# Mamba block on one core: a convolution tap and the carried columns on VectorE, x copied by ScalarE, two of sixteen products on GpSimd, jobs placed anew

## The chip, the cores and the metric

One core of a Trainium2 chip. The metric is the device time of one execution in microseconds (us), from the core's first to its last instruction and what lies around it. Names: TensorE (PE, its weight loads PEld), VectorE (DVE), ScalarE (ACT), GpSimd (POOL), SyncE (SP, which issues all DMAs of the part discussed here).

## What is computed

The program runs layer norms, a two-layer Mamba block, a slot-routing feed-forward, windowed attention and the feed-forward again, on two sequences of 2048 tokens with 256 features. Only the Mamba block is touched. Cut to what matters:

```
xc, z = split(x @ in_w.T)                                    # 512 + 512 features
xc = silu(sum(xp[:, k:k+L] * cw[:, k] for k in range(4)) + cb)   # causal convolution, 4 taps
dt, B, C = split(xc @ xp_w.T)                                # 16, 16, 16
dt = softplus(dt @ dtp_w.T + dtp_b);  A = -exp(A_log)
h[t] = exp(dt[t] * A) * h[t-1] + (dt[t] * xc[t]) * B[t]      # 512 features x 16 states
y[t] = sum_n h[t] * C[t] + xc[t] * D;  out = (y * silu(z)) @ out_w.T
```

## The kernel before

The Mamba part (function `mamba`) works in 16 steps: 2 layers x 2 sequences x 4 chunks of 512 tokens. The 512 x 16 states of a chunk are cut into 64 **units** of 128 partitions (32 features x 4 states) x 512 tokens. For each unit `u`, in this order on each engine:

- ScalarE makes `decay` = exp(A dt) (`decay`, L522; four slots, so it may lead the scans by four units).
- TensorE transposes four 128x128 blocks of `u_B` = (dt x) B into one of two PSUM banks (`inject`, L755).
- VectorE scans over the 512 tokens (`scan`, L406), from `decay` in SBUF and the bank in PSUM, into one of 12 slots of `h`. The scan of unit k of a later chunk begins with column k of `h_carry`.
- GpSimd multiplies the slot by the C rows (`output`, L624).
- TensorE sums the states of four units, a **quad**, into a PSUM bank (`states`, L764), 11 units behind.

`u_B` itself comes from 16 products per 16 units (`product`): 13 on ScalarE (L545) and 3 on GpSimd (L613).

All other work of a step is hung between the units. Each engine's program is one loop `for k in range(UNITS)`, and tuples at the head of the file say behind which unit a job stands: `D_...` for VectorE, `A_...` ScalarE, `G_...` GpSimd, `P_...` TensorE. In step s (p = s + 1) these jobs finish step s-1 (gate, out projection, residual) and prepare the inputs of step s+1 in one chain: norm, transposed features, `project_x`, copy of x out of PSUM (L482), convolution (three taps as products with diagonal weights on TensorE, L678; the newest tap and the sum on VectorE, L350), SiLU (L493), x_proj (L708), `dt_B_C` copy (L507), dt products (L726), softplus (L511, L514), then for four token blocks the transposes of x (L735) and dt (L744), the copy of x to `u_tok` (`tok_x`, L372) and its product with dt (`tok_u`, L377). ScalarE needs a table load (ACT_TABLE_LOAD) when it turns between exp, SiLU and softplus.

After each quad ScalarE copies the four last columns of the scans' slots to `h_carry` (`keep`, L530); GpSimd waits for this copy before it overwrites the quad. All order between engines is by semaphores; each engine takes its instructions strictly in the written order.

Of the kernel before, what the change touches and what calls it, by code (L numbers as in the profile page):

```python
# [63 lines left out]
D_GATE = (62, 63, 4, 7)  # L64
D_RES = (13, 16)
D_STATS = (6, 6, 6, 10)
D_MEAN = 11
# [8 lines left out]
A_NORM = 15
A_FEAT = 20
A_X = (25, 28, 34, 39)
A_PROJ = 43
# [1 line left out]
D_RAW = (11, 12, 13, 14, 28, 38, 39)
G_PROD = (0, 4, 7)
G_RSTD = 5
P_Z = (0, 1, 2, 4, 5, 6, 6, 7)
P_SKIP = (0, 11, 12, 17)
P_OUT = (9, 9, 10, 11, 13, 14, 15, 16)
P_FEAT = 18
P_X = (20, 21, 22, 23, 29, 31, 32, 33)
# [43 lines left out]
def mamba(nc, x, r, weights, consts):  # L132
# [7 lines left out]
    with ExitStack() as ctx:  # L140
# [65 lines left out]
        with nc.Block() as block:  # L206
# [101 lines left out]
            def _(dve):  # L308
# [37 lines left out]
                def conv(p, ct):  # L346
                    at(dve, "conv_mm", CT * p + ct + 1)
                    if ct == 0:
                        at(dve, "skip_mm", CT * p)
                    dve.scalar_tensor_tensor(xc[:, ct], xs[:, ct, DC - 1:], kc(p, K_CW, ct * DC + DC - 1),  # L350
                                             PS[:, conv_bank(p, ct)], ALU.mult, ALU.add).then_inc(S["conv"], 1)
# [1483 lines left out]
```

## Time and profile before

| | |
|---|---|
| median of 3 runs | 2516.12 us (2514.9 to 2517.61) |
| profiled execution, its own time | 2518.79 us |
| its span, first to last instruction | 2517.0 us |
| busy in the span | TensorE 87%, VectorE 75%, ScalarE 72%, GpSimd 64% |
| mean granted TensorE clock | 0.956 of full speed |

In the profile a line names engine, source line, operation, the tile written and the tiles read. Records of TensorE's 512-column fp32 products come in pairs, two to a product. The number at a row's start in a timeline is its start in us from the span's start, the next its length; "x4" means four instructions merged, the length is then that of all four together. "[0.29 <-PE psum L755]" is idle time ahead of it and what ended it.

### The profile page before, as it was taken

How to read it: one execution, taken by the hardware profiler on the slowest of the kernel's cores; microseconds unless marked ns; L12 is line 12 of the kernel's file. 1: busy time of each engine (PE TensorE's matmuls, PEld its weight loads, DVE VectorE, ACT ScalarE, POOL GpSimd, SP SyncE). 2: the span in 40 equal slices, each digit the busy share in tenths (PEclk: the TensorE clock that was granted, in tenths of full speed). 3: DMA queues.
4: the chain of work that ended last, by engine and by line, in shares of the span. 5: the costliest groups of instructions: out<-in, count | busy, mean ns of one | idle time of the engine just before them, and what ended most of it. 6: DMA issues, size and time to landing. Idle time of an engine off the chain costs nothing. (4 is left out here: it accounts for less than half of the span.)

```text
span 2517.0 us, 40372 instructions
## 1 busy us (share of the span) xinstructions
PE 2185.7 (87%) x14544; PEld 1308.8 (52%) x14544; DVE 1895.6 (75%) x2590; ACT 1819.2 (72%) x3103; POOL 1619.7 (64%) x1410
## 2 busy tenths in 40 slices
PE   5789899898998989889898898986368699999967
PEld 2445455454554545545455454553134477787844
DVE  5688889888898888988889898898374455555553
ACT  2888998889989889888888989887252244444452
POOL 1689889898898988989889898899210411231010
PEclk9899999999999999999999999999578799999988
DMA  5540414314143240432404224040501211110031
GB/s 169 123 106 22 118 43 93 96 32 118 42 94 87 78 118 30 114 77 51 118 16 119 66 61 111 17 118 9 190 1 62 65 33 33 29 33 25 21 116 67
DMA packets 129787, 183.73 MB, mean 73 GB/s; under 512 B 14002, under 2 KB 75954, under 8 KB 129204
## 3 DMA queue, kind: packets, MB, share of 16 engines
q1 hardware_dynamic: 129588, 181.16, 26.8%
q8 instruction: 115, 1.88, 0.3%
q14 instruction: 84, 0.69, 0.1%
HBM read 134.45 MB, written 42.47 MB: 70 GB/s over the span
## 5 line engine op out<-in xcount | busy, mean ns | idle before, releaser
L624 POOL TENSOR_TENSOR h<-h,C_rep 128x512 f32<-128x512 f32 x1024 | 1275.9, 1283 | 202.4 <-ACT h_carry L530 202.4
L406 DVE TENSOR_TENSOR_SCAN h<-decay,h_carry,psum 128x512 f32<-128x512 f32 x768 | 955.8, 1270 | 126.4 <-PE psum L755 93.6
L522 ACT ACTIVATE decay<-dt_rep,A 128x512 f32<-128x512 f32 x1024 | 729.3, 713 | 103.6 <-DVE h L406 93.0
L755 PEld LDWEIGHTS psum<-ident,u_B 128*128 128x128 f32 x4096 | 479.1, 142 | 562.5 <-DVE h L406 310.3
L755 PE MATMUL psum<-ident,u_B 128*128 128x128 f32 x4096 | 632.5, 281 | 141.5 <-DVE h L406 109.4
L545 ACT ACTIVATE u_B<-u_tok,B_tok 128x512 f32<-128x512 f32 x832 | 589.0, 709 | 64.3 <-PE psum L755 46.6
L406 DVE TENSOR_TENSOR_SCAN h<-decay,zero,psum 128x512 f32<-128x512 f32 x256 | 319.0, 1271 | 57.2 <-PE psum L755 35.9
L764 PE MATMUL psum<-h,state_sum 128*32 128x512 f32 x2048 | 281.5, 623 | 11.7 <-POOL h L624 11.4
L1600 ACT ACTIVATE a_probs_T<-a_psum 128x512 f32<-128x512 f32 x128 | 76.4, 597 | 197.2 <-PE a_psum L1684 197.2
L613 POOL TENSOR_TENSOR u_B<-u_tok,B_tok 128x512 f32<-128x512 f32 x192 | 200.7, 1045 | 13.5 <-DVE u_tok L377 13.5
L1542 DVE TENSOR_REDUCE a_row_max<-a_psum 128x4 f32<-128x512 f32 x128 | 88.4, 691 | 143.3 <-PE a_psum L1675 143.3
L678 PE MATMUL psum<-x_dt_gated,tap_diag 128*128 128x512 f32 x384 | 189.2, 597 | 0.0
L1469 POOL COPY a_v_skewed<-a_v_tile 64x1088 f32<-64x1088 f32 x8 | 8.7, 1085 | 211.5 <-DVE a_v_tile L1508 211.5
L1675 PE MATMUL a_psum<-a_k,a_q_by_head 128*64 128x128 f32 x2048 | 140.1, 279 | 0.0
L1675 PEld LDWEIGHTS a_psum<-a_k,a_q_by_head 128*64 128x64 f32 x2048 | 109.2, 136 | 52.7 <-issue 52.7
L657 PE MATMUL psum<-h_feat,w_x 128*128 128x512 f32 x256 | 135.0, 613 | 1.0 <-ACT h_feat L472 1.0
L657 PE MATMUL psum<-h_feat,w_z 128*128 128x512 f32 x256 | 132.3, 609 | 1.7 <-ACT silu_z L501 1.7
L779 PE MATMUL psum<-w_out,x_dt_gated 128*128 128x256 f32 x512 | 132.0, 388 | 0.9 <-issue 0.9
L779 PEld LDWEIGHTS psum<-w_out,x_dt_gated 128*128 128x128 f32 x512 | 91.8, 194 | 30.7 <-issue 22.3
L950 POOL TENSOR_TENSOR f_rstd<-f_vareps,f_minushalf 128x8 f32<-128x8 f32 x12 | 21.7, 1808 | 125.5 <-DVE f_vareps L977 125.5
L1547 DVE TENSOR_TENSOR a_probs<-a_psum,a_row_max 128x512 f32<-128x512 f32 x128 | 88.5, 692 | 4.4
L1604 ACT ACTIVATE a_probs<-a_probs 128x512 f32<-128x512 f32 x128 | 79.6, 622 | 8.0 <-DVE a_probs L1547 7.9
(204 smaller groups left out, 2843.4 us busy)
## 6 DMA issues: line engine op xcount, KB each, us to landing
dt_rep<-dt_rows SPq DMA_DIRECT2D x256, 256.0 KB, 5.5
C_rep<-C_rows SPq DMA_DIRECT2D x256, 64.0 KB, 2.0
dt_rows<-x_dt_gated SPq DMA_DIRECT2D x32, 512.0 KB, 4.9
residual<-mamba_residual SPq DMA_DIRECT2D x16, 512.0 KB, 4.0
mamba_residual<-residual SPq DMA_DIRECT2D x16, 512.0 KB, 2.9
x_tok<-mamba_residual SPq DMA_DIRECT2D x15, 512.0 KB, 4.4
f_gru_weights<-in_slot_gru_dram SPq DMA_DIRECT2D x2, 2176.0 KB
u_B<-in_x_dram SPq DMA_DIRECT2D x8, 512.0 KB, 9.4
```

Source lines behind the costliest of these rows:

```text
L406: dve.tensor_tensor_scan(h[:, slot(u)], dec[:, u % DEC], PS[:, u % 2], first, ALU.mult, ALU.add)\
L522: act.activation(dec[:, u % DEC], dtr[:, k % EG], ACT.Exp, scale=A[:, s // STEPS, k:k + 1]).then_inc(S["decay"], 1)
L545: act.activation(pr[:, f % 2, tb, :, EW * n:EW * (n + 1)], uT[:, tb].rearrange("p (g e) -> p g e", e=EW), ACT.Copy, scale=BT[:, p % 2, tb, ...
L613: pool.tensor_tensor(pr[:, f % 2, tb, :, EW * n:EW * (n + 1)], uT[:, tb].rearrange("p (g e) -> p g e", e=EW), BT[:, p % 2, tb, SG * ng + n ...
L624: pool.tensor_tensor(h[:, slot(u)], h[:, slot(u)], crep[:, k // EG], ALU.mult).then_inc(S["hc"], 1)
L657: return pe.matmul(PS[:, bank], w[:, kt, ct * P:(ct + 1) * P], hT[:, kt], start=(kt == 0), stop=(kt == KT - 1))
L678: ins = pe.matmul(PS[:, conv_bank(p, ct)], TAPS[:, ct, j - 1], xs[:, ct, DC - 1 - j:DC - 1 - j + T], start=(j == 1), stop=(j == DC - 1))
L755: ins = pe.transpose(PS[:, u % 2, tb * P:(tb + 1) * P], pr[:, f % 2, tb, eg], ident[:])
L764: ins = pe.matmul(PS[EW * q:EW * (q + 1), YB + j % CT], sely[:], h[:, slot(q0 + q)], start=False, stop=(j >= QUADS - CT))
L779: ins = pe.matmul(PS[:, PA_ + i // 2, i % 2 * D:(i % 2 + 1) * D], g[:, ct, i * P:(i + 1) * P], WO[:, ct], start=(ct == 0), stop=(ct == CT ...
L1547: dve.tensor_tensor(pr[:, n % 4], PS[:, n % 2].rearrange("p (h t) -> p h t", h=4), mx[:, n % 2].rearrange("p (h o) -> p h o", o=1).to_broa ...
L1675: ins = pe.matmul(PS[WIN * blk:WIN * (blk + 1), n % 2, i * P:(i + 1) * P], qS[:, k, h, at:at + WIN], keys, start=False, stop=(i == 3))
```

## The change

- The oldest convolution tap leaves TensorE (two taps stay, `TAPS_PE`). VectorE adds it in a second instruction per feature block, from the two SBUF tiles `x_dt_gated` and `conv_out`, counted by a new semaphore `conv_a`/`conv`.
- `keep` moves from ScalarE to VectorE, behind the first scan of the next quad, and is left out in a sequence's last chunk, where nobody reads it; GpSimd then waits for the scans themselves.
- `tok_x` moves from VectorE to ScalarE.
- Products on GpSimd: 2 of 16 instead of 3.
- Nearly all tuples that place the jobs have new numbers.

```diff
+TAPS_PE = 2
-ON_POOL = (3, 7, 11)
+ON_POOL = (5, 11)
...
-D_CONV = (27, 30, 37, 38)
+D_CONV = (29, 29, 32, 33, 38, 38, 38, 38)
...
-P_CONV = (24, 25, 25, 27, 28, 30, 34, 36, 37, 38, 38, 38)
+P_CONV = (28, 29, 31, 32, 36, 38, 38, 38)
...
-                def conv(p, ct):
+                def conv(p, ct, part):
+                    if part == 1:
+                        at(dve, "conv_a", CT * p + ct + 1)
+                        dve.scalar_tensor_tensor(xc[:, ct], xs[:, ct, 0:T], kc(p, K_CW, ct * DC), xc[:, ct], ALU.mult, ALU.add)\
+                            .then_inc(S["conv"], 1)
+                        return
...
-                def tok_x(p, tb):
-                    at(dve, "xcT_mm", TB * p + tb + 1)
...
-                    dve.tensor_copy(uT[:, tb], PS[:, PB_]).then_inc(S["xcT"], 1)
...
+                def keep(q):
+                    if not 0 <= q < ALL * QUADS or last_chunk(q):
+                        return
+                    at(dve, "scan", QT * (q + 1))
+                    k = QT * (q % QUADS)
+                    dve.tensor_copy(carry[:, k:k + QT], h[:, slot(QT * q):slot(QT * q) + QT, T - 1]).then_inc(S["carry"], 1)
...
+                        if k % QT == 0:
+                            keep((s * UNITS + k) // QT - 1)
...
-                    act.activation(carry[:, k:k + QT], h[:, slot(QT * q):slot(QT * q) + QT, T - 1], ACT.Copy)\
-                        .then_inc(S["carry"], 1)
+                def tok_x(p, tb):
+                    at(act, "xcT_mm", TB * p + tb + 1)
...
+                    act.activation(uT[:, tb], PS[:, PB_], ACT.Copy).then_inc(S["xcT"], 1)
...
                 def output(s, k):
                     u = s * UNITS + k
                     if k % QT == 0:
-                        at(pool, "carry", u // QT + 1)
+                        if last_chunk(u // QT):
+                            at(pool, "scan", u + QT)
+                        else:
+                            at(pool, "carry", carries(u // QT) + 1)
```

The order of instructions at three places, each in the first step that scans. First VectorE, from unit 31 of the kernel before to its unit 42 (L406 is the scan, L350 the convolution):

```order
L406 SCALAR_TENSOR_TENSOR h<-decay,zero,psum 128x512 x7
L350 SCALAR_TENSOR_TENSOR conv_out<-x_dt_gated,small,psum 128x512
L406 SCALAR_TENSOR_TENSOR h<-decay,zero,psum 128x512
L350 SCALAR_TENSOR_TENSOR conv_out<-x_dt_gated,small,psum 128x512
L406 SCALAR_TENSOR_TENSOR h<-decay,zero,psum 128x512 x4
L364 COPY B_tok<-psum 128x64
```

The same place after the change (L420 scan, L364 and L358 the two parts of the convolution, L409 the last columns, L378 B_tok):

```order
L409 COPY h_carry<-h 128x4
L420 SCALAR_TENSOR_TENSOR h<-decay,zero,psum 128x512 x2
L364 SCALAR_TENSOR_TENSOR conv_out<-x_dt_gated,small,psum 128x512
L358 SCALAR_TENSOR_TENSOR conv_out<-x_dt_gated,small,conv_out 128x512
L364 SCALAR_TENSOR_TENSOR conv_out<-x_dt_gated,small,psum 128x512
L358 SCALAR_TENSOR_TENSOR conv_out<-x_dt_gated,small,conv_out 128x512
L420 SCALAR_TENSOR_TENSOR h<-decay,zero,psum 128x512 x2
L409 COPY h_carry<-h 128x4
L420 SCALAR_TENSOR_TENSOR h<-decay,zero,psum 128x512 x2
L378 COPY B_tok<-psum 128x64
```

The third and fourth feature block now stand together behind unit 38, four instructions with no scan between. Second ScalarE, from the SiLU of the convolution on, before (L493 and L496 SiLU, L507 the copy of dt, B, C, L522 decay, L530 last columns, L545 product):

```order
L493 ACTIVATE conv_out<-conv_out,small 128x512 x4
L496 ACTIVATE silu_z<-silu_z 128x2048
L522 ACT_TABLE_LOAD
L522 ACTIVATE decay<-dt_rep,A 128x512
L507 ACTIVATE dt_B_C<-psum 64x512
L530 ACTIVATE h_carry<-h 128x4
L522 ACTIVATE decay<-dt_rep,A 128x512
```

and after the change (the same operations are at L506, L509, L520 and L535):

```order
L506 ACTIVATE conv_out<-conv_out,small 128x512 x4
L509 ACTIVATE silu_z<-silu_z 128x2048
L520 ACTIVATE dt_B_C<-psum 64x512
L535 ACT_TABLE_LOAD
L535 ACTIVATE decay<-dt_rep,A 128x512 x2
```

The copy of dt, B and C stands ahead of the table load now. Third VectorE from unit 44 to unit 51, where the token blocks are made, before (L357 raw dt, L372 copy of x, L377 product with dt):

```order
L357 TENSOR_SCALAR x_dt_gated<-psum,small 128x512 x2
L406 SCALAR_TENSOR_TENSOR h<-decay,zero,psum 128x512 x3
L372 COPY u_tok<-psum 128x512
L377 TENSOR_TENSOR u_tok<-psum,u_tok 128x512
L406 SCALAR_TENSOR_TENSOR h<-decay,zero,psum 128x512
L372 COPY u_tok<-psum 128x512
L406 SCALAR_TENSOR_TENSOR h<-decay,zero,psum 128x512
L377 TENSOR_TENSOR u_tok<-psum,u_tok 128x512
L406 SCALAR_TENSOR_TENSOR h<-decay,zero,psum 128x512 x2
L372 COPY u_tok<-psum 128x512
```

and after (L371 raw dt, L384 the product):

```order
L371 TENSOR_SCALAR x_dt_gated<-psum,small 128x512 x2
L420 SCALAR_TENSOR_TENSOR h<-decay,zero,psum 128x512
L409 COPY h_carry<-h 128x4
L420 SCALAR_TENSOR_TENSOR h<-decay,zero,psum 128x512 x3
L384 TENSOR_TENSOR u_tok<-psum,u_tok 128x512
L420 SCALAR_TENSOR_TENSOR h<-decay,zero,psum 128x512
L409 COPY h_carry<-h 128x4
L384 TENSOR_TENSOR u_tok<-psum,u_tok 128x512
L420 SCALAR_TENSOR_TENSOR h<-decay,zero,psum 128x512 x2
L384 TENSOR_TENSOR u_tok<-psum,u_tok 128x512
```

The copies of x are gone from VectorE, and the first product stands one scan later.

## Rows read from the trace of the kernel before

**Rows 1.** The page, busy us and share of the span by engine.

```profile
PE 2185.7 (87%) x14544; PEld 1308.8 (52%) x14544; DVE 1895.6 (75%) x2590; ACT 1819.2 (72%) x3103; POOL 1619.7 (64%) x1410
```

**Rows 2.** VectorE in order of time, first and last scan of the Mamba part.

```profile
78.29 2.50 DVE L406 TENSOR_TENSOR_SCAN h<-decay,zero,psum 128x512 f32<-128x512 f32 x2 [11.34 <-ACT decay L522]
...
1760.17 1.27 DVE L406 TENSOR_TENSOR_SCAN h<-decay,h_carry,psum 128x512 f32<-128x512 f32 x1
```

**Rows 3.** Stretches of one step: us; busy PE, PEld, DVE, ACT, POOL; clock, DMA, GB/s.

```profile
715.49:777.66 62.17, 62.17 (x334) 35.63 (x336) 54.88 (x56) 54.55 (x97) 59.73 (x53) 1.00 0.12 32
777.66:797.93 20.27, 17.72 (x100) 8.88 (x92) 14.54 (x17) 20.05 (x29) 10.25 (x10) 1.00 0.32 105
797.93:820.86 22.93, 16.71 (x114) 9.30 (x112) 22.93 (x25) 20.14 (x37) 22.93 (x20) 1.00 0.79 169
sum 105.37, PE 96.60 PEld 53.81 DVE 92.36 ACT 94.73 POOL 92.91; mean PE 32.20 PEld 17.94 DVE 30.79 ACT 31.58 POOL 30.97
```

**Rows 4.** Waits of VectorE and GpSimd: us in total, times, longest.

```profile
DVE h L406 <- PE psum L755: 129.6, 149, 3.0
...
POOL h L624 <- ACT h_carry L530: 202.4, 67, 22.5
```

**Rows 5.** TensorE in order of time, within the first stretch.

```profile
747.87 0.60 PE L755 MATMUL psum<-ident,u_B 128*128 128x128 f32 x4
748.30 1.02 PE L657 MATMUL psum<-h_feat,w_x 128*128 128x512 f32 x2
749.16 0.60 PE L755 MATMUL psum<-ident,u_B 128*128 128x128 f32 x4
...
774.22 2.74 PE L678 MATMUL psum<-x_dt_gated,tap_diag 128*128 128x512 f32 x6
```

**Rows 6.** VectorE in order of time, in the same step.

```profile
774.39 0.72 DVE L350 SCALAR_TENSOR_TENSOR conv_out<-x_dt_gated,small,psum 128x512 f32<-128x512 f32 x1
775.03 1.27 DVE L406 TENSOR_TENSOR_SCAN h<-decay,h_carry,psum 128x512 f32<-128x512 f32 x1
...
802.06 0.67 DVE L372 COPY u_tok<-psum 128x512 f32<-128x512 f32 x1
...
812.63 5.96 DVE L406 TENSOR_TENSOR_SCAN h<-decay,h_carry,psum 128x512 f32<-128x512 f32 x5
```

**Rows 7.** ScalarE and VectorE in order of time, in the second stretch.

```profile
783.69 1.28 ACT L522 ACT_TABLE_LOAD   x1
...
785.61 0.57 ACT L507 ACTIVATE dt_B_C<-psum 64x512 f32<-64x512 f32 x1
...
789.98 1.28 ACT L511 ACT_TABLE_LOAD   x1
...
794.23 0.69 DVE L372 COPY u_tok<-psum 128x512 f32<-128x512 f32 x1 [0.86 <-PE psum L735]
794.80 0.72 ACT L522 ACTIVATE decay<-dt_rep,A 128x512 f32<-128x512 f32 x1
795.03 0.69 DVE L377 TENSOR_TENSOR u_tok<-psum,u_tok 128x512 f32<-128x512 f32 x1
795.43 0.71 ACT L545 ACTIVATE u_B<-u_tok,B_tok 128x512 f32<-128x512 f32 x1
```

**Rows 8.** Groups of instructions: busy us, mean ns of one, idle before.

```profile
L624 POOL TENSOR_TENSOR h<-h,C_rep 128x512 f32<-128x512 f32 x1019 | 1269.8, 1283 | 202.4 <-ACT h_carry L530 202.4
...
L613 POOL TENSOR_TENSOR u_B<-u_tok,B_tok 128x512 f32<-128x512 f32 x189 | 197.6, 1045 | 0.0
...
L530 ACT ACTIVATE h_carry<-h 128x4 f32<-128x4 f32 x256 | 49.7, 194 | 4.6 <-DVE h L406 4.6
```

**Rows 9.** VectorE and GpSimd in order of time, feed-forward behind the Mamba part.

```profile
1811.25 1.64 POOL L950 TENSOR_TENSOR f_rstd<-f_vareps,f_minushalf 128x8 f32<-128x8 f32 x1 [14.93 <-DVE f_vareps L977]
1811.57 0.17 DVE L1055 TENSOR_SCALAR f_slot_mean<-f_slot_mean 128x2 f32<-128x2 f32 x1
...
1816.49 2.29 DVE L993 TENSOR_TENSOR f_x<-f_x,f_norm_w_b 128x2048 f32<-128x2048 f32 x1
1816.65 3.62 POOL L950 TENSOR_TENSOR f_rstd<-f_vareps,f_minushalf 128x8 f32<-128x8 f32 x1 [3.48 <-DVE f_vareps L977]
```

More of the change, by code:

```diff
@@ L61 @@
 K_ALL = K_LNB + KT
[L64 to L67, printed above, removed]
-D_CONV = (27, 30, 37, 38)
+D_GATE = (63, 63, 5, 9)
+D_RES = (19, 20)
+D_STATS = (3, 6, 8, 12)
+D_MEAN = 14
+D_CONV = (29, 29, 32, 33, 38, 38, 38, 38)
 D_DT = (43, 43)
 D_B = 42
-D_XT = (46, 47, 50, 54)
-D_U = (46, 48, 51, 57)
-A_Z = (5, 6, 9, 15)
+D_U = (47, 48, 50, 57)
+A_Z = (3, 8, 10, 17)
 A_SILU = 42
 A_HALO = 42
[L76 to L79, printed above, removed]
+A_NORM = 21
+A_FEAT = 23
+A_X = (27, 31, 37, 39)
+A_PROJ = 42
 A_SP = 46
[L81 to L88, printed above, removed]
-P_CONV = (24, 25, 25, 27, 28, 30, 34, 36, 37, 38, 38, 38)
-P_PROJ = (41, 41, 41, 41)
+A_XT = (47, 48, 50, 56)
+D_RAW = (14, 15, 16, 17, 30, 34, 39)
+G_PROD = (7, 7)
+G_RSTD = 11
+P_Z = (0, 1, 2, 4, 5, 8, 9, 11)
+P_SKIP = (1, 6, 9, 21)
+P_OUT = (12, 13, 14, 16, 17, 18, 20, 20)
+P_FEAT = 22
+P_X = (24, 25, 26, 30, 33, 34, 34, 37)
+P_CONV = (28, 29, 31, 32, 36, 38, 38, 38)
+P_PROJ = (41, 41, 42, 42)
 P_B = 43
-P_DT = (43, 43, 45, 45)
-P_XT = (47, 48, 50, 53)
-P_DTT = (47, 49, 51, 57)
+P_DT = (43, 43, 44, 46)
+P_XT = (47, 48, 50, 52)
+P_DTT = (47, 49, 50, 52)
 class Signals:
@@ L188, in mamba @@
         names = ("x0_stats x0_var x0_rstd r0 r0_st r0_st2 const zero x_ld r_ld r_st c_st dt_st dt_st2 w_x w_z w_o w_p w_dt w_skip w_taps A_exp A half stats rs nm xh tp hT x_mm "
-                 "x_ev conv_mm conv halo xp_mm dbl silu z_mm z_ev sz dt_mm dt_raw dt bt_mm bt xcT_mm xcT dtT_mm uT skip_mm decay "
+                 "x_ev conv_mm conv_a conv halo xp_mm dbl silu z_mm z_ev sz dt_mm dt_raw dt bt_mm bt xcT_mm xcT dtT_mm uT skip_mm decay "
                  "b scan carry hc ysum prod_a prod_p gated o_mm res").split()
@@ L350, in conv @@
                     dve.scalar_tensor_tensor(xc[:, ct], xs[:, ct, DC - 1:], kc(p, K_CW, ct * DC + DC - 1),
[L351 removed]
+                                             PS[:, conv_bank(p, ct)], ALU.mult, ALU.add).then_inc(S["conv_a"], 1)
                 def raw_dt(p, ct):
@@ L403, in scan @@
                         if s % CHUNKS:
-                            at(dve, "carry", u // QT - QUADS + 1)
+                            at(dve, "carry", carries(u // QT - QUADS) + 1)
                     first = carry[:, k:k + 1] if s % CHUNKS else zero[:]
@@ L439, in _ @@
                             if k == D_CONV[n]:
-                                conv(p, n)
+                                conv(p, n // 2, n % 2)
                         for n in range(len(D_DT)):
@@ L578, in _ @@
                             softplus(p)
+                        for n in range(len(A_XT)):
+                            if k == A_XT[n]:
+                                tok_x(p, n)
             @block.gpsimd
@@ L664, in project_x @@
                             at(pe, "hT", KT * (p + 1))
-                        at(pe, "conv", CT * p + ct - 1 if ct >= 2 and p else 0)
+                        at(pe, "conv_a", CT * p + ct - 1 if ct >= 2 and p else 0)
                     ins = project(x_bank(p, ct), WX, ct, kt)
@@ L807, in _ @@
                                 project_x(p, n // KT, n % KT)
-                        for n in range(CT * (DC - 1)):
+                        for n in range(CT * TAPS_PE):
                             if k == P_CONV[n]:
-                                conv(p, n // (DC - 1), n % (DC - 1) + 1)
+                                conv(p, n // TAPS_PE, n % TAPS_PE + 1)
                         for n in range(CT):
```

25 lines of the change are left out of this document (10 added, 15 removed).

## The prediction

> **What bounds the kernel now.** I read the page's busy shares first: TensorE 87%, VectorE 75%, ScalarE 72%, GpSimd 64% [rows 1]. These are means over parts with different limits, so the next view is a division of one step. The scans of the Mamba part start at 78.29 us, and the last of the 1024 starts at 1760.17 us and takes 1.27 us [rows 2]; that is 1683 us for 16 steps, 105.2 us each. The 754 us after it run code that the diff leaves alone. One step (span 715.49 to 820.86 us, 105.37 us) cut at scan 39 and at scan 48 gives three stretches [rows 3]:
> - A, scans 0 to 38, 62.17 us. TensorE is busy 62.17 of them, VectorE 54.88. TensorE is the bound.
> - B, scans 39 to 47, 20.27 us. No engine that scans is full; ScalarE is busy 20.05. This is the serial chain that prepares the next step.
> - C, scans 48 to 63, 22.93 us. VectorE is busy 22.93, TensorE only 16.71. VectorE is the bound.
>
> The waits say the same: VectorE's scans wait for TensorE's `u_B` transposes 149 times, 129.6 us in all [rows 4]. In A the pattern is visible one pair at a time. Four transposes take 0.43 us (747.87 to 748.30) and the 128x512 product behind them 0.86 us (to 749.16), together 1.29 [rows 5], while five scans in a row take 5.96 us, the last 1.27, so 1.17 us from start to start [rows 6]. Two PSUM banks hold the scans' input, so a TensorE job longer than 0.74 us ahead of a transpose group is seen by the scans one or two units later.
>
> **Part by part, for one step.** *Tap to VectorE.* One product of two records lasts 1.02 us, three taps of six records 2.74 [rows 5]: 0.86 us for each further one. Four taps leave TensorE, all of them in A: -3.44 us. VectorE receives four instructions with two SBUF tensors. There is no row for this form at 128x512 in the Mamba part; the same instruction with one PSUM input takes 0.64 us from start to start (774.39 to 775.03) and 0.72 us by itself [rows 6]; 0.58 (a plain copy, below) and 0.72 bound it. I take 0.64, plus 0.1 us where it stands right behind the instruction that it depends on (the dependent pair `u_tok` copy and product leaves 0.11 us: 794.23 + 0.69 to 795.03) [rows 7]. At units 29, 32 and 33 this lies beside TensorE's work (units 31 and 34 each carry two jobs). At unit 38 all of ct 2 and ct 3 now stands behind one scan: 1.17 + 4 x 0.64 + 0.35 = 4.1 us, where TensorE needs 0.43 + 3 x 0.86 = 3.0. So 1.1 us is uncovered, and the next step's SiLUs wait for it. A: -3.44 + 1.1 = -2.3 us; bounds -3.4 (the lump hidden) and -1.
>
> *Last columns to VectorE.* ScalarE loses 16 copies of 0.19 us [rows 8], VectorE gets 12 per step on average (the last chunk of four has none). The nearest row is a 128x2 tensor_scalar from SBUF to SBUF, 0.17 us [rows 9]. VectorE's instructions overlap their neighbour by 0.1 us (1.27 against 1.17), so the bounds for one are 0.07 and 0.17, and I take 0.1, nearer to the first, as neighbours overlap everywhere in these rows. In A they lie under TensorE. In C, where VectorE is the bound, 4 x 3/4 x 0.1 = +0.3 us. GpSimd reads the last columns' semaphore before it may multiply a quad; today it waits 202.4 us in all for ScalarE's copy [rows 4], mostly in B, where GpSimd is busy 10.25 of 20.27 us [rows 3]; it has caught up there and the wait costs nothing.
>
> *x to ScalarE.* Four 128x512 copies of `u_tok` leave VectorE, three of them in C: 0.67 us each [rows 6], 0.58 with the overlap, so -1.7. ScalarE pays about 0.5 us for each (its 512-column copy `dt_B_C` out of PSUM takes 0.57, neighbours overlapping by 0.1) [rows 7]. C: -1.7 + 0.3 = -1.4 us, now 21.5.
>
> *Products.* ScalarE takes 14 of 16 instead of 13: +4 x 0.61 us (decay and product alternate at 0.61: 794.80, 795.43) [rows 7]. GpSimd loses 4 x 1.05 [rows 8].
>
> *B, the chain.* Before: SiLUs, a table load of 1.28 us at 783.69, a decay, the `dt_B_C` copy at 785.61, the softplus load at 789.98, and after softplus the first decay at 794.80 [rows 7]. After: the `dt_B_C` copy stands ahead of the table load, so B_tok and dt start some 1.3 us earlier, but the decay of unit 43 comes 1.2 us later, and up to the softplus stand four decays and three products, 7 x 0.61 = 4.3 us, behind a copy and a load of 1.9 us: softplus 0.4 to 0.6 us later than now. The first `u_tok` copy then comes behind decay and product, at 796.0 instead of 794.23; but scan 47 now stands ahead of the `u_tok` product, so 1.2 us of that is covered. I take B as +0.4 us, between -1 and +2.
>
> *Everything else moved* (z, skip, w_out, norm, x, residual): in A it only spreads TensorE's jobs. Before, TensorE's unit 11 holds three jobs beside its transposes (state sums, skip, w_out); afterwards no unit of A but 38 holds more than two. I price that at nothing and keep -1 us per step as the lower end. No DMA is added or moved past another on SP's queue. Before the first scan four taps fewer on a chain that ends in a wait for dt_rep: -1.5 us, between -3 and 0.
>
> **The sum.** -2.3 + 0.4 - 1.4 = -3.3 us per step, 16 times -53, with the start -54. The profiled execution took 2518.8 us (span 2517.0), the median of the runs is 2516.1, so 2.7 lower. 2518.8 - 54 - 2.7 = 2462 us, 2.2% less.
>
> **The rule that speaks against it.** What the trace shows of VectorE and GpSimd working in SBUF at the same time [rows 9]: a power of 128x8 on GpSimd takes 1.64 us at 1811.25, and 3.62 us at 1816.65, where VectorE had begun a 2.29 us tensor_tensor with two SBUF inputs 0.16 us earlier. The 128x2 tensor_scalar of 1811.57 runs its 0.17 us in the middle of a power. So in these rows VectorE keeps its time and GpSimd pays. Priced so, GpSimd loses 4 x 0.64 + 12 x 0.1 = 3.8 us per step and wins 4.2 by the products: nothing on the path. That is my forecast's reading.
>
> The Trainium skill, SBUF — State Buffer, section Who interferes with whom, says more: a VectorE instruction with two SBUF inputs, or a copy that may use both ports, and a GpSimd instruction that reads SBUF exclude each other for the whole instruction, and whoever issues first holds the port. The rows agree for the case in which VectorE is first; none shows VectorE behind a streaming GpSimd instruction. By that rule the rival below would be the outcome.
>
> **Rivals.** *VectorE waits for GpSimd (slower).* Place: the four `conv` second parts and the 12 last-column copies, each behind a running `h<-h,C_rep` of 1.24 us (its mean of 1.28 less the overlap of its neighbour) [rows 8]. GpSimd is busy 59.73 of 62.17 us in A and all of C [rows 3]. A wait of half an instruction, 0.6 us, 16 times, is 9.6 us per step; half of the copies may find GpSimd idle, since it waits for this very copy, and a quarter of the rest may hide under TensorE: 4 x 0.6 + 6 x 0.6 = 6.0, times 0.75 = 4.5 us against the gain of 3.4. That is +1.2 per step: 2462 + 16 x 4.5 = 2534 us. With nothing hidden 2462 + 154 = 2616. It decides from 0.21 us per instruction on (3.4 / 16). For it: two engines on one port is what rows 9 show. Against: VectorE's times there never change. If a smaller part shows (under 0.2 us each) the time is 2480 to 2510.
>
> *ScalarE becomes the bound (smaller gain).* It is busy 94.73 of 105.37 us [rows 3] and gets 4 x 0.61 + 4 x 0.5 - 16 x 0.1 = +2.8: 97.5 of 102. In C its pair of decay and product needs 1.22 us where a scan needs 1.17. If its lead of four decays is used up, A's gain halves and C's goes: -1.5 per step, 2490 us.
>
> *The lump at unit 38 eats the gain.* If the pairs of dependent instructions cost 0.3 us apart and unit 29's is seen too, A gains 1 us only: 2482 us, a part of the main case's range.
>
> **Chances.** Forecast (2440 to 2488, its own range) 0.52; shared port with a small part 0.13; shared port that decides, 2515 to 2600, 0.22; ScalarE's bound 0.10; other mishaps 0.03. A measurement here tells 0.2%, 5 us, from no change. Faster by more than that: 0.52 + 0.10 + nearly all of 0.13 = 0.72; within it 0.06; slower 0.22. The range leaves out the far half of the slower rival and the best ends: 2440 to 2556.
>
> **What would show it.** In the new profile: tap records 256 instead of 384; stretch A near 60 us with TensorE still full; one scan after the four conv instructions of unit 38 about 4.1 us behind the scan before; C near 21.5 us with VectorE full; a step of 102. The second conv parts at 0.7 us and the last-column copies under 0.2 with the next scan directly behind them. Wrong, if these last two take 1 us and more or if VectorE shows gaps ahead of them that no engine's semaphore ends; wrong too if ScalarE's decays end most of the scans' waits in A or C.

## The result and the profile after

The changed kernel takes 2545.89 us (median of 4 runs, 2545.46 to 2547.38) against 2516.35 us for the kernel before, measured beside it: ratio 1.0119, 95% interval 1.0101 to 1.0136. It is 1.2% slower, where 2.2% faster was forecast. The stated range of 2440 to 2556 us holds the time only through its part for the slower rival; the forecast's own range, 2440 to 2488, doesn't.

The page of the changed kernel, busy us by engine (before: [rows 1]):

```profile
PE 2177.1 (86%) x14416; PEld 1290.0 (51%) x14416; DVE 1968.6 (77%) x2782; ACT 1855.7 (73%) x2975; POOL 1577.4 (62%) x1346
```

TensorE lost 128 records (two for each tap that left) and only 8.6 us of busy time, though four taps per step left it. VectorE grew by 73 us. Two of its instruction forms take far longer than they should. The groups of instructions by form show them, restricted to the tiles of the convolution and of the last columns (number, then shortest/median/longest in ns, then the first start and the last):

```profile
L364 DVE SCALAR_TENSOR_TENSOR conv_out<-x_dt_gated,small,psum x64: 710/723/747, 33.2 to 1655.3; 128x512 f32<-128x512 f32 x64
L358 DVE SCALAR_TENSOR_TENSOR conv_out<-x_dt_gated,small,conv_out x64: 751/1338/4305, 33.9 to 1656.1; 128x512 f32<-128x512 f32 x64
L409 DVE COPY h_carry<-h x192: 134/146/956, 84.5 to 1704.9; 128x4 f32<-128x4 f32 x192
```

The first convolution part (one input in PSUM) never takes more than 0.75 us. The second (both inputs in SBUF, same size) takes up to 4.3 us, and a copy of 128x4 elements up to 0.96. No semaphore is awaited there: the time stands inside the instruction. The page gives the second part's sum, 90.1 us for 64, so 1.41 each:

```profile
L358 DVE SCALAR_TENSOR_TENSOR conv_out<-x_dt_gated,small,conv_out 128x512 f32<-128x512 f32 x64 | 90.1, 1407 | 1.7
```

Put VectorE's and GpSimd's order of time side by side, at unit 33 and at unit 29 of the next step:

```profile
777.89 1.26 DVE L420 TENSOR_TENSOR_SCAN h<-decay,h_carry,psum 128x512 f32<-128x512 f32 x1
779.09 1.37 DVE L358 SCALAR_TENSOR_TENSOR conv_out<-x_dt_gated,small,conv_out 128x512 f32<-128x512 f32 x1
...
771.86 10.96 POOL L640 TENSOR_TENSOR h<-h,C_rep 128x512 f32<-128x512 f32 x8
...
880.95 4.30 DVE L358 SCALAR_TENSOR_TENSOR conv_out<-x_dt_gated,small,conv_out 128x512 f32<-128x512 f32 x1
...
879.68 5.02 POOL L640 TENSOR_TENSOR h<-h,C_rep 128x512 f32<-128x512 f32 x4
887.70 2.51 POOL L640 TENSOR_TENSOR h<-h,C_rep 128x512 f32<-128x512 f32 x2 [2.99 <-DVE h L420]
```

The second part (the tap) that starts at 880.95 ends at 885.25, 0.55 us behind the end of GpSimd's fourth instruction (884.70). It started when the second of the four did (four take 5.02 us, so one starts every 1.25 us). Its own work takes less than 0.75 us, so it did next to none before: it waited through three whole instructions. At 779.09 it got in behind one, and now GpSimd paid too: its eight instructions, between which two second parts got in, last 10.96 us, not the 10.07 of eight others in this step.

The pattern is the same throughout the trace. All 54 second parts in the Mamba steps that take over 0.75 us end 0.54 to 0.55 us behind the end of a GpSimd instruction. Where GpSimd had more to do, its next instruction took 1.72 to 1.76 us instead of 1.28. Which GpSimd instruction a second part gets in behind differs even at one place: at unit 29 it takes 1.9 us in most steps, and 4.3 in three, all of them last-chunk steps.

One step cut as in [rows 3] (scans 39 and 48 of the step at 727.46, and of the next, a last-chunk step without column copies):

```profile
727.46:790.02 62.56, 61.11 (x336) 34.77 (x334) 60.81 (x69) 55.15 (x90) 56.70 (x48) 1.00 0.10 29
790.02:811.93 21.91, 17.95 (x82) 7.90 (x83) 13.21 (x16) 19.34 (x25) 11.92 (x10) 0.92 0.31 98
811.93:836.69 24.76, 18.98 (x117) 10.72 (x116) 23.35 (x26) 22.58 (x38) 21.91 (x18) 0.86 0.81 167
836.69:902.01 65.32, 62.27 (x334) 35.30 (x333) 61.70 (x60) 55.34 (x90) 55.73 (x48) 0.97 0.20 63
902.01:922.58 20.57, 17.00 (x86) 7.80 (x85) 13.12 (x14) 19.34 (x25) 12.36 (x11) 1.00 0.30 100
922.58:944.77 22.20, 17.20 (x123) 10.14 (x122) 22.00 (x22) 22.08 (x37) 20.44 (x18) 1.00 0.79 165
```

A is no shorter than before the change, and in the last-chunk step, with its 4.3 us tap, 3 us longer. In the ordinary step B and C are 1.3 and 2.6 us longer than in the last-chunk step, and there the granted TensorE clock is 0.92 and 0.86 instead of 1.00.

### The profile page after: what moved, and what is told of

The parts are those of the page before. It is cut to its first block and busy times, and to the rows that moved or that the text cites. A ratio compares the mean times of both kernels' runs of the same rounds, so it can differ in the third digit from the quotient of the medians.

```text
span 2545.5 us, 40051 instructions
## 1 busy us (share of the span) xinstructions
PE 2177.1 (86%) x14416; PEld 1290.0 (51%) x14416; DVE 1968.6 (77%) x2782; ACT 1855.7 (73%) x2975; POOL 1577.4 (62%) x1346
## 5 line engine op out<-in xcount | busy, mean ns | idle before, releaser
L640 POOL TENSOR_TENSOR h<-h,C_rep 128x512 f32<-128x512 f32 x1024 | 1291.4, 1298 | 285.6 <-DVE h_carry L409 224.8
L420 DVE TENSOR_TENSOR_SCAN h<-decay,h_carry,psum 128x512 f32<-128x512 f32 x768 | 949.9, 1266 | 106.1 <-PE psum L771 56.7
L771 PE MATMUL psum<-ident,u_B 128*128 128x128 f32 x4096 | 659.1, 286 | 184.4 <-DVE h L420 143.0
L535 ACT ACTIVATE decay<-dt_rep,A 128x512 f32<-128x512 f32 x1024 | 724.6, 715 | 62.0 <-DVE h L420 56.6
L557 ACT ACTIVATE u_B<-u_tok,B_tok 128x512 f32<-128x512 f32 x896 | 637.1, 712 | 59.0 <-PE psum L771 54.9
L420 DVE TENSOR_TENSOR_SCAN h<-decay,zero,psum 128x512 f32<-128x512 f32 x256 | 315.8, 1264 | 38.4 <-ACT decay L535 24.9
L780 PE MATMUL psum<-h,state_sum 128*32 128x512 f32 x2048 | 296.2, 653 | 5.4 <-POOL h L640 5.4
L626 POOL TENSOR_TENSOR u_B<-u_tok,B_tok 128x512 f32<-128x512 f32 x128 | 131.1, 1048 | 15.3 <-DVE u_tok L384 15.3
L694 PE MATMUL psum<-x_dt_gated,tap_diag 128*128 128x512 f32 x256 | 128.9, 607 | 0.7 <-ACT x_dt_gated L495 0.7
L358 DVE SCALAR_TENSOR_TENSOR conv_out<-x_dt_gated,small,conv_out 128x512 f32<-128x512 f32 x64 | 90.1, 1407 | 1.7
```

The lines of the kernel that those rows point to most:

```text
L358: dve.scalar_tensor_tensor(xc[:, ct], xs[:, ct, 0:T], kc(p, K_CW, ct * DC), xc[:, ct], ALU.mult, ALU.add)\
L420: dve.tensor_tensor_scan(h[:, slot(u)], dec[:, u % DEC], PS[:, u % 2], first, ALU.mult, ALU.add)\
L535: act.activation(dec[:, u % DEC], dtr[:, k % EG], ACT.Exp, scale=A[:, s // STEPS, k:k + 1]).then_inc(S["decay"], 1)
L557: act.activation(pr[:, f % 2, tb, :, EW * n:EW * (n + 1)], uT[:, tb].rearrange("p (g e) -> p g e", e=EW), ACT.Copy, scale=BT[:, p % 2, tb, ...
L626: pool.tensor_tensor(pr[:, f % 2, tb, :, EW * n:EW * (n + 1)], uT[:, tb].rearrange("p (g e) -> p g e", e=EW), BT[:, p % 2, tb, SG * ng + n ...
L640: pool.tensor_tensor(h[:, slot(u)], h[:, slot(u)], crep[:, k // EG], ALU.mult).then_inc(S["hc"], 1)
```

## Experiments

The kernels differ from the changed kernel only by the edits shown or named. Each was timed with the kernel before beside it, so the ratios compare better than the times do. Stretches are means over steps 1 to 14 (of 0 to 15), from the starts of the scans in each trace. "Tap" is the mean duration of the second convolution part, "columns" that of the h_carry instruction on VectorE, in ns; a field is empty where VectorE has no such instruction.

| kernel | us | ratio to before (95%) | A | B | C | tap | columns |
|---|---|---|---|---|---|---|---|
| before | 2516 | 1 | 62.52 | 20.26 | 23.07 | | |
| changed | 2545.9 | 1.0119 (1.0101-1.0136) | 62.97 | 21.33 | 24.21 | 1407 | 286 |
| t1 tap through PSUM | 2500.7 | 0.9945 (0.9928-0.9963) | 61.51 | 20.57 | 23.49 | 741 | 324 |
| t2 columns by reduction | 2552.5 | 1.0154 (1.0131-1.0178) | 66.34 | 20.56 | 22.39 | 2002 | 132 |
| t3 both | 2474.0 | 0.9839 (0.9819-0.9859) | 60.48 | 20.57 | 22.45 | 742 | 133 |
| t4 columns on ScalarE | 2538.8 | 1.0097 (1.0082-1.0113) | 62.40 | 21.46 | 24.35 | 1326 | |
| t5 tap on TensorE | 2509.0 | 0.9966 (0.9951-0.9982) | 62.30 | 20.57 | 23.17 | | 282 |
| t7 = t3, 3 products | 2480.0 | 0.9865 (0.9845-0.9885) | 61.03 | 20.57 | 22.38 | 742 | 133 |
| t8 = t3, x on VectorE | 2515.8 | 0.9997 (0.9982-1.0012) | 60.40 | 21.36 | 24.81 | 742 | 133 |
| t9 = t3, tap on TensorE | 2496.6 | 0.9928 (0.9911-0.9945) | 62.34 | 20.57 | 22.43 | | 133 |
| t10 = t3, dt_B_C later | 2453.1 | 0.9759 (0.9740-0.9777) | 60.47 | 19.57 | 22.43 | 742 | 133 |
| t11 = t10, tensor_scalar | 2491.2 | 0.9896 (0.9877-0.9916) | 61.34 | 19.57 | 23.57 | 741 | 321 |
| t12 = t10, columns on ScalarE | 2486.3 | 0.9879 (0.9859-0.9898) | 60.93 | 19.66 | 23.81 | 742 | |
| t13 = t2, GpSimd paced | 2508.6 | 0.9960 (0.9942-0.9977) | 63.19 | 21.04 | 22.36 | 1555 | 133 |

**The tap through PSUM (t1).** The first part writes its sum back into the PSUM bank it read, and the second reads it there. TensorE's `project_x` then waits for the second part.

```diff
-dve.scalar_tensor_tensor(xc[:, ct], xs[:, ct, DC - 1:], ..., PS[:, conv_bank(p, ct)], ALU.mult, ALU.add)...
+dve.scalar_tensor_tensor(PS[:, conv_bank(p, ct)], xs[:, ct, DC - 1:], ..., PS[:, conv_bank(p, ct)], ALU.mult, ALU.add)...
-dve.scalar_tensor_tensor(xc[:, ct], xs[:, ct, 0:T], ..., xc[:, ct], ALU.mult, ALU.add)...
+dve.scalar_tensor_tensor(xc[:, ct], xs[:, ct, 0:T], ..., PS[:, conv_bank(p, ct)], ALU.mult, ALU.add)...
```

> The kernel after, but the first part of the convolution leaves its sum in the PSUM bank and the second part reads it from there, so no VectorE instruction has two SBUF tensors; TensorE then waits for the second part before it uses the bank again. Theory P (VectorE's instructions with two SBUF operands wait for GpSimd's running instruction): the 64 second parts fall from 1.41 us to about 0.73 us each, 42 us in all, three quarters of it on the path or more: 2505 to 2516 us. Rival S (the new places of the jobs cost the time, the longer instructions are hidden under TensorE): the second parts get shorter but the time stays within 5 us of 2546.

2500.7 us, 45 below the changed kernel and 4 below theory P's range; rival S is out. The same instruction with one input in PSUM, at the same place, never waits. The groups by form of t1:

```profile
L358 DVE SCALAR_TENSOR_TENSOR conv_out<-x_dt_gated,small,psum x64: 714/748/751, 33.0 to 1616.6; 128x512 f32<-128x512 f32 x64
L409 DVE COPY h_carry<-h x192: 135/146/941, 85.0 to 1662.6; 128x4 f32<-128x4 f32 x192
```

**The columns by a reduction (t2), and both (t3).**

```diff
-dve.tensor_copy(carry[:, k:k + QT], h[:, slot(QT * q):slot(QT * q) + QT, T - 1])...
+dve.tensor_reduce(carry[:, k:k + QT], h[:, slot(QT * q):slot(QT * q) + QT, T - 1:T], AX, ALU.max)...
```

> The kernel after, but VectorE copies the four last columns with a reduction over an axis of one element instead of a copy. Theory P, with the copy in a mode that takes both of VectorE's ports: 192 copies fall from a mean of 0.286 to about 0.14 us, 28 us in all, most of it where VectorE is full: 2520 to 2530 us. Rival (it is the SBUF-to-SBUF access by itself, or the wait for the scan's last columns): the instruction keeps lengths up to 0.9 us and the time stays at 2546.

> Both of the above. Theory P: 2475 to 2492 us, the forecast's main case (2462) plus what its chain of stretch B was short by (about 0.9 us per step). Rival S: over 2530 us.

In t2 the columns take 0.13 us each time and C falls to 22.39, so the rival (they stay long) is out. But the kernel is at 2552.5 us, 22 us or more above theory P's range: the tap of unit 29 now takes 5.5 us in most steps, where it took 1.9.

```profile
L358 DVE SCALAR_TENSOR_TENSOR conv_out<-x_dt_gated,small,conv_out x64: 723/1063/5829, 32.6 to 1672.3; 128x512 f32<-128x512 f32 x64
L409 DVE TENSOR_REDUCE h_carry<-h x192: 122/132/136, 83.5 to 1717.4; 128x4 f32<-128x4 f32 x192
```

With both waits gone (t3) the kernel takes 2474.0 us, 72 less than the changed kernel, 1 below theory P's range and within 12 us of the forecast 2462. The two removals are not additive (45 less and 7 more by themselves, 72 together; the 7 are small beside the spread of t2's runs, 2548.0 to 2558.2). The mean of the tap rose from 1.41 to 2.00 us when the columns stopped waiting, that of the columns from 0.29 to 0.32 when the tap did. The reading is that each wait shifts VectorE against GpSimd and so changes what the other finds.

**The columns back on ScalarE (t4).** `keep` is written as before the change, except that it is still left out in the last chunks.

> The kernel after, with the last columns copied by ScalarE again, at the units of the kernel before (still left out in a last chunk); the tap stays as in the kernel after. Theory P: VectorE loses its 55 us of copies, 28 of them waits; ScalarE gets 192 x 0.1 us. 2515 to 2530 us, a little better or equal to the reduction if ScalarE is not the bound. Rival (ScalarE has become the bound): slower than the run with the reduction by over 5 us, with more scans waiting for decay.

2538.8 us: better than the changed kernel by 7 us, and 14 better than t2, so the rival is out. P's range is missed by 9 us. The tap waits nearly as long as in the changed kernel (mean 1.33 us, in three last-chunk steps 5.4), and C stays at 24.35 without any copy on VectorE, so taking the copies' waits away gave nothing there. What holds C is seen in t12.

**The tap back on TensorE, with the copy (t5) and with the reduction (t9).**

```diff
-TAPS_PE = 2
+TAPS_PE = 3
-D_CONV = (29, 29, 32, 33, 38, 38, 38, 38)
+D_CONV = (29, 32, 38, 38)
-P_CONV = (28, 29, 31, 32, 36, 38, 38, 38)
+P_CONV = (28, 29, 29, 31, 32, 32, 36, 37, 38, 38, 38, 38)
```

> The changed kernel with the oldest tap on TensorE again; the last columns stay a copy on VectorE. The kernel with the tap on TensorE and the columns by a reduction took 0.9928 of before. If the 192 copies wait by themselves (theory: a copy from SBUF to SBUF waits for GpSimd's running instruction), this one is slower than that by the 26 us that the copies cost beside the tap through PSUM: 2520 to 2530 us, mean copy near 0.32 us. Rival: the copies are only late because the tap's waits upset the order of VectorE and GpSimd; then 2495 to 2505 us and a mean copy under 0.2 us.

> The kernel without either port wait (2474 us, 0.984 of before), with the oldest tap on TensorE again, so that this tap alone is undone: conv instructions of VectorE at units 29, 32, 38, 38. By the prediction's term for A (four taps of 0.86 us less, 1.1 us more at unit 38) the time rises by 16 x 2.3 = 37 us to 2511 us, stretch A from 60.5 to 62.8. Rival: the new placement and not the tap carries A's gain; then the time stays under 2485 us.

t5, without the oldest tap on VectorE, keeps the copy's mean of 282 ns: the copies wait by themselves, which settles against the rival. The time, 2509.0 us, lies between the two ranges. The price of the copies is smaller than expected, since they cost 0.7 us in C but nothing in A, where TensorE is full again. t9 measures the tap alone: A 62.34 against t3's 60.48, 1.9 us per step. The time lies between the expected 2511 and the rival's 2485: the tap is worth 22 us by the ratios and 28 by the spans of the profiled executions (2495.3 and 2467.0), where 37 were expected. A's whole gain from before to t3 is 2.0 us, so the tap and not the placement carries it.

**Three products on GpSimd (t7), x on VectorE (t8), dt_B_C one unit later (t10), all on t3.**

```diff
 # t7
-ON_POOL = (5, 11)
+ON_POOL = (3, 7, 11)
-G_PROD = (7, 7)
+G_PROD = (0, 4, 7)
 # t8: tok_x on VectorE again, at the units of A_XT
-act.activation(uT[:, tb], PS[:, PB_], ACT.Copy).then_inc(S["xcT"], 1)
+dve.tensor_copy(uT[:, tb], PS[:, PB_]).then_inc(S["xcT"], 1)
 # t10
-A_PROJ = 42
+A_PROJ = 43
```

> This is the kernel without either port wait (tap through PSUM, last columns by a reduction; 2474 us, 0.984 of before), with three of sixteen products on GpSimd again, as before. In it stretch C measured 22.45 us where the forecast said 21.5. Theory 1 (ScalarE's lead of decays is used up at the end of a step, it bounds C): ScalarE loses 4 x 0.61 us, 0.6 of it in C, so C falls by 0.3 to 0.6 us and the whole to 2464 to 2470 us. Theory 2 (GpSimd, which is full in A and C, bounds C): it gets 1.05 us more per sixteen units, and the time rises by 16 x 0.5 to 16 x 2 us, to 2482 to 2505 us. Within 5 us of 2474: neither.

> The kernel without either port wait (2474 us, 0.984 of before), with the four copies of x to u_tok on VectorE again, at the same units. By the term of the prediction three copies of 0.58 us come back into C, where VectorE is full: C 22.45 + 1.7 = 24.2 us, +27 us in all, 2501 us. If ScalarE or GpSimd bounds C now, the copies fit beside them, and the time stays within 5 us of 2474 or falls.

> The kernel without either port wait (2474 us, 0.984 of before), with the copy dt_B_C one unit later on ScalarE, behind the table load and the decay of unit 43 as before the change. By the prediction's reading the copy ahead of the load lets B_tok and dt start 1.3 us earlier but costs the softplus 0.4 to 0.6 us. If the chain to the softplus bounds stretch B, B stays within 0.5 us (2466 to 2482 us). If B_tok and dt bound it, B rises by 1 us or more: 2490 us and above.

t7: 6 us more, C unchanged (22.38), A 0.55 us longer. Neither theory's bound of C is confirmed; the intervals of t3 and t7 overlap, and it stays open.

t8: 0.9997, so x on ScalarE is worth 1.6%, 40 us, more than the 27 expected. C rises by 2.4 us and B by 0.8. Two stretches C of t8 show a part of the price that is not VectorE's work:

```profile
800.81:826.68 25.87, 20.27 (x120) 12.19 (x119) 24.28 (x29) 21.80 (x35) 21.67 (x18) 0.83 0.81 171
1545.91:1570.26 24.35, 17.91 (x124) 10.10 (x122) 24.10 (x30) 21.44 (x35) 20.41 (x17) 1.00 0.78 172
```

The same work takes 24.35 us at clock 1.00 and 25.87 at 0.83. Against the 22.34 us of one of t3's stretches C (shown in the next part), three copies cost 2.0 us at full clock, 0.67 each; I had priced 0.58.

t10: neither case came: no change, or a slower kernel, had been expected, and B falls by 1.0 us in every step and the kernel to 2453.1 us, the fastest here, 2.4% below before. ScalarE in order of time, first t3, then t10:

```profile
762.05 1.89 ACT L509 ACTIVATE silu_z<-silu_z 128x2048 f32<-128x2048 f32 x1
764.84 0.59 ACT L520 ACTIVATE dt_B_C<-psum 64x512 f32<-64x512 f32 x1 [0.89 <-PE psum L724]
765.45 1.28 ACT L535 ACT_TABLE_LOAD   x1
```

```profile
757.83 1.89 ACT L509 ACTIVATE silu_z<-silu_z 128x2048 f32<-128x2048 f32 x1
759.74 1.28 ACT L535 ACT_TABLE_LOAD   x1
761.03 0.72 ACT L535 ACTIVATE decay<-dt_rep,A 128x512 f32<-128x512 f32 x1
761.66 0.57 ACT L520 ACTIVATE dt_B_C<-psum 64x512 f32<-64x512 f32 x1
```

In t3 the copy, right behind SiLU, waits 0.89 us for x_proj, which itself needed the SiLU's output; the table load stands behind it. In t10 load and decay run during that wait. ScalarE is busy 19.34 of B's 20.57 us in t3 and 19.23 of 19.57 in t10, so the time that it no longer stands idle is what B lost.

**What kind of instruction waits (t11, on t10).**

```diff
-dve.tensor_reduce(carry[:, k:k + QT], h[:, slot(QT * q):slot(QT * q) + QT, T - 1:T], AX, ALU.max)...
+dve.tensor_scalar(carry[:, k:k + QT], h[:, slot(QT * q):slot(QT * q) + QT, T - 1], 1.0, None, ALU.mult)...
```

> The fastest kernel so far (tap through PSUM, dt_B_C copy one unit later, 2453 us, 0.976 of before) with the last columns written by a tensor_scalar (times 1.0) in place of the reduction; input and output are the same SBUF columns. If what waits is the kind of instruction named COPY, this does not wait: mean 0.13 us, 2450 to 2458 us. If any one-input elementwise instruction from SBUF to SBUF waits and only the reduction does not, the mean is near 0.32 us, and the time 2470 to 2485 us.

```profile
L409 DVE TENSOR_SCALAR h_carry<-h x192: 138/145/1298, 83.5 to 1645.3; 128x4 f32<-128x4 f32 x192
```

Mean 321 ns, longest 1.3 us, and 38 us more than t10 (34 by the ratios; 6 above the range of the theory that had the mean right): a tensor_scalar waits like a copy; the reduction does not. The Trainium skill, SBUF — State Buffer, section Who interferes with whom, says the same of the kinds: copies and tensor_scalar may take the shared port pair, tensor_reduce on trn2 never does. The trace agrees (0.14 us longest against 0.96 and 1.30).

t11 also has two stretches C with the same work at either clock. Their four column instructions take the same in both, 0.14, 0.14, 0.30 and 0.87 us in the first and within 0.01 of that in the second:

```profile
574.12:597.39 23.27, 17.22 (x123) 10.16 (x122) 23.17 (x27) 22.55 (x38) 20.59 (x17) 1.00 0.80 172
783.00:807.77 24.77, 19.00 (x117) 10.81 (x116) 23.47 (x26) 22.73 (x38) 21.90 (x18) 0.86 0.82 178
```

**Who gains from the early columns (t12, on t10).** `keep` on ScalarE at its old units, two quads later than on VectorE.

> The fastest kernel so far (2453 us, 0.976 of before) with the last columns on ScalarE at their old units (64 steps' worth of them still left out in the last chunks). Neither engine waits for the other in SBUF then, so this weighs only where 12 copies of 0.19 us per step stand. ScalarE is full in B, where two or three of them fall: B + 0.3 to 0.5 us, C and A between -0.3 (VectorE loses four instructions of 0.1 us) and +0.3: 2450 to 2462 us. If ScalarE's lead of decays bounds C, C rises by 0.5 us and more: 2462 to 2475 us.

33 us more than t10 (30 by the ratios), beyond either expectation. Stretches B and C of one step, t10 and then t12:

```profile
753.72:773.28 19.57, 16.91 (x86) 7.79 (x85) 13.14 (x16) 19.23 (x25) 11.91 (x10) 1.00 0.32 107
773.28:795.63 22.35, 17.20 (x123) 10.14 (x122) 22.20 (x26) 22.23 (x37) 19.80 (x17) 1.00 0.79 161
```

```profile
764.55:784.24 19.68, 16.94 (x86) 7.82 (x85) 13.05 (x14) 19.42 (x27) 8.70 (x8) 1.00 0.34 108
784.24:808.36 24.12, 17.95 (x121) 10.55 (x120) 22.27 (x22) 23.09 (x42) 22.91 (x20) 0.93 0.70 152
```

GpSimd (fifth engine column) does 8.70 us of work in B instead of 11.91, since it gets its quads later, and is then busy 22.91 of 24.12 us in C. TensorE's state sums wait for its `h` 33 us in all, in t10 5. ScalarE's decays are not what holds C: over the stretches C of steps 1 to 14 the scans wait for them 0.17 us per step, for TensorE 1.26 (in t10 no wait of this kind is over 0.1 us). So the early release of the quads was worth more than the copies cost. No VectorE instruction of t12 waits for GpSimd inside itself, and still the clock of its C falls to 0.86 in two of the 14 steps and to 0.93 in four.

**GpSimd paced (t13, on t2).**

```diff
+at(pool, "scan", min(u + QT + 1, ALL * UNITS))
 pool.tensor_tensor(h[:, slot(u)], h[:, slot(u)], crep[:, k // EG], ALU.mult)
```

> The kernel with the reduction and the tap between two SBUF tiles (2552 us, 1.015 of before), in which the tap waited through up to 4 or 5 GpSimd instructions back to back (mean 2.0 us, longest 5.83). Here GpSimd's multiplication of each unit also waits for the scan five units on, so that it gets its work one unit at a time instead of a quad at a time; the reach of the wait is the only edit. Theory: the tap gets in only when GpSimd stands at a semaphore, so its wait ends after the released instructions are used up; now that is one or two: longest tap under 3.3 us, mean under 1.4 us, and the time falls by 64 x 0.6 = 40 us to about 2515 us, if the pace itself costs nothing. Rival: VectorE loses some other fixed contest at those places; then the longest stays above 4 us and the time at 2545 us or more.

The time falls by 44 us to 2508.6 (49 by the ratios), as the theory had it. The tap's mean falls less than expected, to 1.56 us, and its longest to 4.36, which is above the 4 us of the rival: unit 29's takes 3.83 in most steps instead of 5.46. In t2, then in t13:

```profile
667.80 5.46 DVE L358 SCALAR_TENSOR_TENSOR conv_out<-x_dt_gated,small,conv_out 128x512 f32<-128x512 f32 x1
...
665.76 2.05 POOL L626 TENSOR_TENSOR u_B<-u_tok,B_tok 128x512 f32<-128x512 f32 x2
667.76 4.96 POOL L640 TENSOR_TENSOR h<-h,C_rep 128x512 f32<-128x512 f32 x4
677.19 1.28 POOL L640 TENSOR_TENSOR h<-h,C_rep 128x512 f32<-128x512 f32 x1 [4.47 <-DVE h_carry L409]
```

```profile
655.11 3.83 DVE L358 SCALAR_TENSOR_TENSOR conv_out<-x_dt_gated,small,conv_out 128x512 f32<-128x512 f32 x1
...
655.88 2.52 POOL L641 TENSOR_TENSOR h<-h,C_rep 128x512 f32<-128x512 f32 x2
660.22 3.75 POOL L641 TENSOR_TENSOR h<-h,C_rep 128x512 f32<-128x512 f32 x3 [1.82 <-DVE h L420]
```

In both the tap ends about 0.55 us behind the last instruction that GpSimd had been released for, in t2 behind four multiplications, in t13 behind the end of a product and two. So at unit 29 of these two kernels the theory holds; my numbers for it were too good. It is not the whole rule: other taps (779.09 above) get in behind one instruction while GpSimd has more, and why is not settled.

## Why the prediction failed, by its own steps

- **The bounds** of A and C were right. Where no port wait disturbs (t3), TensorE is busy 59.64 of 60.14 us in A, and VectorE 22.19 of 22.34 in C:

```profile
697.80:757.94 60.14, 59.64 (x330) 34.00 (x329) 57.95 (x70) 54.88 (x91) 57.30 (x50) 1.00 0.16 38
757.94:778.51 20.57, 16.99 (x86) 7.79 (x85) 13.21 (x16) 19.34 (x25) 11.93 (x10) 1.00 0.32 105
778.51:800.85 22.34, 17.20 (x123) 10.14 (x122) 22.19 (x26) 22.23 (x37) 19.80 (x17) 1.00 0.79 165
```

- **The step that failed** is the reading of [rows 9]: "So in these rows VectorE keeps its time and GpSimd pays. Priced so, GpSimd loses ..." and the prices that follow, 0.64 us for the tap and 0.1 for the columns from start to start (0.72 and 0.17 by themselves). Measured by themselves: 1.41 and 0.29 us, where forms that don't wait take 0.74 (t1) and 0.13 (t2). Those rows show GpSimd at 128x8 powers, never at back-to-back 128x512 multiplications, and VectorE either first or without a conflict; they are no case of the one that mattered. The rival was built on that case; what was put against it, that VectorE's times never change, came from rows without it. The 128x2 tensor_scalar that ran in the middle of a power says nothing of one beside a multiplication of 512 columns: in t11 such an instruction takes up to 1.30 us.
- **The rival that came about** is "VectorE waits for GpSimd", forecast at 4.5 us per step and 2534 us. Measured in the same unit: 4 x (1.407 - 0.741) + 12 x (0.286 - 0.133) = 4.5 us of waits per step, and 108.51 - 103.49 = 5.0 us of step against t3. That the two figures agree is luck. The rival's waits were 6.0 us, of which a quarter was hidden, and its working (half an instruction each) was not how it came: the second parts at unit 29 wait for one to three whole instructions, most copies not at all (median 146 ns). And it left out the clock.
- **The clock** was in no case of the forecast. Where TensorE has waited for late scans or for the SiLU behind the convolution, its granted clock falls from 1.00 (2.4 GHz) to 0.50 (1.2 GHz). Slices of 2 us of the changed kernel, in B and in C:

```profile
790.00:792.00 2.00, 0.66 (x4) 0.42 (x4) 2.00 (x3) 1.84 (x3) 0.00 (x0) 0.96 0.00 0
792.00:794.00 2.00, 1.50 (x3) 0.52 (x3) 1.70 (x3) 2.00 (x4) 1.40 (x2) 0.50 0.00 0
...
824.00:826.00 2.00, 0.93 (x6) 0.69 (x7) 2.00 (x4) 2.00 (x5) 1.89 (x3) 0.99 1.08 214
826.00:828.00 2.00, 2.00 (x12) 0.47 (x10) 2.00 (x3) 2.00 (x4) 2.00 (x2) 0.50 1.08 215
```

  The same work of TensorE, in each pair first at full clock, then where it had fallen (for the second pair, during part of it):

```profile
821.23 1.07 PE L780 MATMUL psum<-h,state_sum 128*32 128x512 f32 x8
826.60 1.93 PE L780 MATMUL psum<-h,state_sum 128*32 128x512 f32 x8
...
796.29 1.93 PE L724 MATMUL psum<-conv_out,w_xproj 128*64 128x512 f32 x4
792.52 3.25 PE L724 MATMUL psum<-conv_out,w_xproj 128*64 128x512 f32 x4 [0.50 <-ACT conv_out L506]
```

  In C most of it comes back as waits of the scans for their transposes; the longest in the stretch at 811.93:

```profile
829.64 1.28 DVE L420 TENSOR_TENSOR_SCAN h<-decay,h_carry,psum 128x512 f32<-128x512 f32 x1 [1.02 <-PE psum L771]
```

  The price by stretches of equal work: 1.5 us in C (24.77 against 23.27 in t11), 1.3 us in B (21.91 against 20.57 here). So of C's 24.76 us, 22.34 are work, about 0.9 the copies' waits, and 1.5 the clock (an estimate from these stretches). That the waits bring the fall about is shown as far as t3 and t10, without them, have B at 1.00 in steps 1 to 14 and C at 1.00 in ten and eleven of them. They are not the only way to it: t12's C falls without any. What tips it in a single step is not shown.
- **Tap**: -3.44 + 1.1 = -2.3 us in A. Without the waits -1.9 (t9 to t3) and -2.0 (before to t3). The lump at unit 38 fits: in t3 four conv instructions stand from 755.06 to the next scan at 757.94, and with the scan before them 2.88 + 1.17 = 4.05 us, forecast 4.1.
- **x to ScalarE**: the term of C said three copies. It was a miscount: [rows 6] and the trace have only two `tok_x` copies behind scan 48 (802.06 and 807.94), the other two lie in B, at 794.23 [rows 7] and 797.32. So C's term of -1.7 should have read -1.2, with +0.3 for the columns 0.9 shorter instead of 1.4; t3's is 0.6 shorter. Undone, the move costs 40 us (t8).
- **Last columns**: their own cost was seen too low only with the copy; by a reduction they take 0.13 us each. "It costs nothing" of the wait for ScalarE's copy was wrong on the other side: taken back to ScalarE the columns cost 33 us (t12), since GpSimd gets its quads later.
- **B**: +0.4 forecast, +0.3 in t3; the number was right by luck, the cause was misread. The early dt_B_C copy was booked as a start 1.3 us earlier; it costs 1.0 us (t10).
- **Start**: -1.5 us forecast, -2.1 measured (first scan at 76.23 instead of 78.29).

With its terms measured without port waits the forecast's sum of -3.3 us per step comes out as -2.4 (t3: 103.49 against 105.86), and 2462 as 2474. The mechanism held for the tap in A, for x in C and for the start; it did not for B and for GpSimd's wait. The waits of two instruction forms, and the clock behind them, cost more than the whole gain.

## What to carry to other kernels

Before work goes to VectorE beside a busy GpSimd, look at the operands: two inputs in SBUF, or a copy or tensor_scalar within SBUF, waited for whole GpSimd instructions here; one input through PSUM, or a reduction over an axis of one element, did not in any of these kernels. A row that shows two engines together prices a conflict only if it shows the same kind of instruction on both sides, in the same order of arrival. And a copy that waits for its own predecessor belongs behind a table load, not ahead of it.

## What was not expected of the hardware

- A waiting VectorE instruction stood through several GpSimd instructions back to back: 4.30 us (three of them), 5.46 us (four), longest 5.83, for a work of 0.75. The Trainium skill, SBUF — State Buffer, section Who interferes with whom, says that whoever issues first holds the port for the whole instruction; by that, one instruction of 1.24 us would be the longest wait (an estimate), and the trace of t2 shows four times as much. When VectorE got in while GpSimd had more to do, the GpSimd instruction behind it lost time as well (1.72 to 1.76 us instead of 1.28).
- Removing one of two conflicts made the other worse (t2: the tap's mean 2.00 us instead of 1.41; the kernel 0.35% slower than the changed kernel by the ratios, whose intervals just overlap), so such waits can't be priced singly.
- Stretches of equal work lost 1.3 to 1.5 us where TensorE's granted clock fell to 0.50, after it had waited for late scans or the late SiLU.
